# Latent attention with maxima computed one half-head ahead: values taken for four key tiles at a time

## The reference, cut to what matters

```python
q = rmsnorm(x @ q_a_w.T, q_a_ln) @ q_b_w.T            # 2048 tokens, 16 heads, 64 + 64 (rope)
ckv = x @ kv_a_w.T                                    # latent c (32) and one shared k_pe (64)
kv = rmsnorm(c, kv_a_ln) @ kv_b_w.T
query = concat([q_nope, rope(q_pe)]); key = concat([k_nope, rope(k_pe)])
scores = einsum('bhsd,bhtd->bhst', query, key) / sqrt(128)
attn = softmax(scores)                                # over all 2048 keys, no mask
out = einsum('bhst,bhtd->bhsd', attn, v)
return out.transpose(0, 2, 1, 3).reshape(B, S, H * VD) @ o_w.T
```

## Time and profile before

| | |
|---|---|
| median of three runs | 2275.55 us (2272.08 to 2276.42) |
| the profiled execution's own time | 2273.43 us |
| its span | 2271.2 us |
| TensorE busy | 2033.0 us, 90% of the span |
| VectorE, ScalarE, GpSimd busy | 1404.6, 1359.6 and 1356.0 us (60 to 62%) |
| mean granted TensorE clock | 0.938 of full |

### The profile page before, as it was taken

How to read it: one execution, slowest core, us unless ns; L and a number is a source line. 1 busy time by engine, 2 the same in 40 slices (tenths; PEclk the granted TensorE clock), 3 DMA queues, 4 the chain that set the end, 5 groups by cost and what they waited for, 6 DMA issues and landing times. The chain is left out here.

```text
span 2271.2 us, 44766 instructions
## 1 busy us (share of the span) xinstructions
PE 2033.0 (90%) x13754; PEld 1328.6 (58%) x13754; DVE 1404.6 (62%) x2973; ACT 1359.6 (60%) x1959; POOL 1356.0 (60%) x799
## 2 busy tenths in 40 slices
PE   5898999999999999999999999999764379999980
PEld 3653666666666666666666666666553257777760
DVE  4545777777776777777776777674242144555547
ACT  2421677777777777777777777778521025555540
POOL 1240678777777777777877778778443703333330
PEclk8886999999999999999999999999876689999995
DMA  4118993000000000000000000000011428999977
GB/s 166 43 44 315 403 400 118 0 0 0 0 0 0 0 0 0 0 0 0 0 0 0 0 0 0 0 0 2 27 59 52 144 78 278 347 337 336 334 265 259
DMA packets 90470, 227.44 MB, mean 100 GB/s; under 512 B 13198, under 2 KB 46904, under 8 KB 90296
## 3 DMA queue, kind: packets, MB, share of 16 engines
q1 hardware_dynamic: 77368, 195.03, 24.4%
q0 software_dynamic: 10752, 29.72, 3.4%
q10 hardware_dynamic: 2304, 2.10, 0.3%
HBM read 125.52 MB, written 101.28 MB: 100 GB/s over the span
## 5 line engine op out<-in xcount | busy, mean ns | idle before, releaser
L688 POOL TENSOR_TENSOR prob_lo<-prob,prob_hi 128x1024 f16<-128x1024 f32 x512 | 1092.5, 2156 | 336.3 <-ACT prob_hi L711 336.3
L760 DVE TENSOR_REDUCE maxes<-ring 128x1 f32<-128x512 f32 x1024 | 648.2, 685 | 245.5 <-PE ring L860 230.4
L709 ACT ACTIVATE prob<-p_s,prob_scale 128x1024 f32<-128x1024 f32 x512 | 571.1, 1115 | 361.9 <-PE p_s L894 361.6
L711 ACT ACTIVATE prob_hi<-p_s,prob_scale 128x1024 f16<-128x1024 f32 x512 | 569.7, 1113 | 0.0
L860 PE MATMUL ring<-kr_hi,qr_hi 64*128 64x512 f32 x1024 | 404.7, 417 | 9.9 <-DVE qc_hi L747 7.0
L860 PE MATMUL ring<-kc_pair,qc_hi 64*128 64x512 f32 x1024 | 387.6, 399 | 0.0
L894 PE MATMUL p_s<-qr_lo,kr_hi 64*128 64x512 f32 x1024 | 298.9, 391 | 0.0
L894 PE MATMUL p_s<-qr_hi,kr_lo 64*128 64x512 f32 x1024 | 297.2, 390 | 0.0
L1157 POOL DMA_INDIRECT ranked_out<-y,dest x128 | 122.6, 958 | 266.3 <-DVE y L1461 263.6
L894 PE MATMUL p_s<-qr_hi,kr_hi 64*128 64x512 f32 x1024 | 280.9, 435 | 0.3 <-ACT prob_hi L711 0.3
L894 PE MATMUL p_s<-qc_lo,kc_one 33*128 33x512 f32 x1024 | 252.9, 392 | 0.0
(11 more groups left out here) (240 smaller groups left out, 2805.6 us busy)
## 6 DMA issues: line engine op xcount, KB each, us to landing
w<-in_experts SPq DMA_DIRECT2D x128, 608.0 KB
expert_rows<-zeros SPq DMA_DIRECT2D x129, 526.0 KB, 9.1
rows<-expert_rows SPq DMA_DIRECT2D x128, 131.5 KB
got<-ranked_out SPq DMA_DIRECT2D x16, 768.0 KB, 11.1
wqb<-in_wqb SPq DMA_DIRECT2D x16, 341.0 KB, 3.0
x<-in_x SPq DMA_DIRECT2D x1, 2048.0 KB, 8.1
cbar<-in_woT SPq DMA_DIRECT2D x1, 2048.0 KB
ranked_out<-y,dest POOLq DMA_INDIRECT x128
```

What stands on the lines that cost most here:

```text
L688: gp.tensor_tensor(prob_lo[s % NB][:, :], prob[s % 2][:, :], prob_hi[s % NB][:, :], ALU.subtract).then_inc(lo_ready, 1)
L709: act.activation(prob[s % 2][:, :], p_s[s % 2][:, :], ACT.Exp, bias=prob_scale[:, :], scale=SCALE)
L711: act.activation(prob_hi[s % NB][:, :], p_s[s % 2][:, :], ACT.Exp, bias=prob_scale[:, :], scale=SCALE).then_inc(p_ready, 1)
L760: v.tensor_reduce(maxes[:, at:at + 1], bank[:, :], AX.X, ALU.max).then_inc(ring_used, 1)
```

## The change

The half-head becomes four groups in place of eight. Group g scores key tiles 4g + 2 to 4g + 5 and then weighs tiles 4g to 4g + 3. The maxima are laid out anew (8 in group 0, from round 8 on, 12 in group 1, 12 in group 2, none in group 3), the groups have 28, 32, 32 and 20 rounds. `turn` moves to round 8 of group 0, amid scores; `rows` to the head of group 3, right behind values; `rope` to round 6 of group 3, amid scores; `rest` stays right ahead of values, now those of tiles 12 to 15. The number of every kind of instruction stays the same, and so do the buffers: two score buffers, three ring banks, eight `prob_hi` and `prob_lo`. The bookkeeping of ring uses is written otherwise, to the same effect.

```diff
-        SLOTS = BATCH * len(PARTS)
-
-        MORE, LESS, NONE = ((0, 4, 7), (2, 5, 9)), ((1, 6), (3, 8)), ((), ())
-        MAX_AT = (MORE, LESS, MORE, MORE, LESS, MORE, NONE, NONE)
+        SLOTS = 4 * len(PARTS)
+
+        MAX_AT = (((8, 11, 14, 17), (10, 12, 15, 19)), ((0, 3, 7, 10, 13, 17), (2, 5, 8, 12, 15, 18)),
+                  ((0, 3, 6, 9, 12, 15), (1, 4, 7, 10, 13, 17)), ((), ()))
...
-                aside = {(1, 0): ("turn", not first), (6, 8): ("rows", more)}.get((g, len(rounds)))
+                aside = {(0, 8): ("turn", not first), (3, 0): ("rows", more), (3, 6): ("rope", after)}.get((g, len(rounds)))
...
-                        now.append(("score", c, BATCH * g + 2 + at[c] // len(PARTS), at[c] % len(PARTS)))
+                        now.append(("score", c, 4 * g + 2 + at[c] // len(PARTS), at[c] % len(PARTS)))
...
-            if after and g in (5, 6):
-                rounds.append([({5: "rope", 6: "rest"}[g], None, None, None)])
...
-                    for kt in range(BATCH * g, BATCH * g + BATCH):
+                    if g == 3 and after:
+                        project_rest(half, use_of(m, "rest"), ring[PLACE["rest"] % RING])
+                    for kt in range(4 * g, 4 * g + 4):
                         weigh(kt, m)
```

More of the change, by code:

```diff
@@ L54 @@
 RING = 3
-BATCH = 2
 class Chain:
@@ L612, in attention @@
                  (kc_one, qc_lo, KR))
-        SLOTS = BATCH * len(PARTS)
-        MORE, LESS, NONE = ((0, 4, 7), (2, 5, 9)), ((1, 6), (3, 8)), ((), ())
-        MAX_AT = (MORE, LESS, MORE, MORE, LESS, MORE, NONE, NONE)
-        BEGUN = [[sum(len(MAX_AT[i][c]) for i in range(g)) for c in range(2)] for g in range(len(MAX_AT))]
+        SLOTS = 4 * len(PARTS)
+        MAX_AT = (((8, 11, 14, 17), (10, 12, 15, 19)), ((0, 3, 7, 10, 13, 17), (2, 5, 8, 12, 15, 18)),
+                  ((0, 3, 6, 9, 12, 15), (1, 4, 7, 10, 13, 17)), ((), ()))
+        BEGUN = [[sum(len(MAX_AT[i][c]) for i in range(g)) for c in range(2)] for g in range(4)]
         def plan(g, first=False, more=True, after=True):
@@ L635, in plan, with use_of @@
                     elif at[c] < SLOTS:
-                        now.append(("score", c, BATCH * g + 2 + at[c] // len(PARTS), at[c] % len(PARTS)))
+                        now.append(("score", c, 4 * g + 2 + at[c] // len(PARTS), at[c] % len(PARTS)))
                         at[c] += 1
                 rounds.append(now)
-            if after and g in (5, 6):
-                rounds.append([({5: "rope", 6: "rest"}[g], None, None, None)])
-            return rounds
[L643 to L657, removed]
+            return rounds
+        MAXIMA = [(c, n) for g in range(4) for now in plan(g) for what, c, n, part in now if what == "max" and part == 1]
+        USES = 2 * MX + 4
+        PLACE = {"turn": 0, "rows": USES - 3, "rope": USES - 2, "rest": USES - 1}
+        PLACE.update({place: 1 + i for i, place in enumerate(MAXIMA)})
+        def use_of(m, what, gone=0):
+            return USES + USES * m + PLACE[what] - gone
         block = st.enter_context(nc.Block())
@@ L713, in head @@
                     if s == 3 and more:
-                        act.wait_ge(ring_mm, use_of(2 * h, "turn")[0] + 1)
+                        act.wait_ge(ring_mm, use_of(2 * h, "turn") + 1)
                         copy_wq(h + 1)
@@ L789, in half_head @@
                 m = 2 * h + half
-                state = (first, more, after)
+                gone = 0 if more else 2
                 if not first:
                     copy_out(m - 1)
-                for g in range(len(MAX_AT)):
+                for g in range(4):
                     for now in plan(g, first, more, after):
@@ L796, in half_head @@
                             if what == "max" and part == 1:
-                                maximum(c, n, m + 1, *use_of(m, (c, n), *state), (c, n) == MAXIMA[-1])
+                                maximum(c, n, m + 1, use_of(m, (c, n)), ring[PLACE[c, n] % RING], (c, n) == MAXIMA[-1])
                             elif what == "turn":
-                                turn(1 - half, h - (1 - half), *use_of(m, "turn", *state))
+                                turn(1 - half, h - (1 - half), use_of(m, "turn", gone), ring[-gone % RING])
                             elif what == "rows":
-                                rows(m + 1, 1 - half, *use_of(m, "rows", *state))
+                                rows(m + 1, 1 - half, use_of(m, "rows"), ring[PLACE["rows"] % RING])
                             elif what == "rope":
-                                project_rope(half, *use_of(m, "rope", *state))
-                            elif what == "rest":
-                                split(m + 2, half, *use_of(m, "rest", *state))
+                                project_rope(half, use_of(m, "rope"), ring[PLACE["rope"] % RING])
+                if after:
+                    split(m + 2, half, use_of(m, "rest"), ring[PLACE["rest"] % RING])
             step(v.tensor_copy(identr[:, :], ident[:, :]))
@@ L826, in _ @@
             copy_out(2 * H - 1)
-            turn(1, H - 1, use_of(2 * H - 1, "turn", more=False)[0] + 1, ring[-1 % RING])
+            turn(1, H - 1, use_of(2 * H - 1, "turn", 1), ring[-1 % RING])
         @block.tensor
@@ L920, in half_head @@
                             elif what == "score" and more:
-                                score(c, n - 16, part, m + 1, 1 - half, use_of(m, "rows", *state)[0])
+                                score(c, n - 16, part, m + 1, 1 - half, use_of(m, "rows"))
                             elif what == "max":
-                                maximum(c, n, part, m + 1, 1 - half, *use_of(m, (c, n), *state))
+                                maximum(c, n, part, m + 1, 1 - half, use_of(m, (c, n)), ring[PLACE[c, n] % RING])
                             elif what == "turn":
-                                turn(m - 1, *use_of(m, "turn", *state))
+                                turn(m - 1, use_of(m, "turn", gone), ring[-gone % RING])
                             elif what == "rows":
-                                rows(m + 1, *use_of(m, "rows", *state))
+                                rows(m + 1, use_of(m, "rows"), ring[PLACE["rows"] % RING])
                             elif what == "rope":
-                                project_rope(h + 1, half, *use_of(m, "rope", *state))
-                            elif what == "rest":
-                                project_rest(half, *use_of(m, "rest", *state))
-                    for kt in range(BATCH * g, BATCH * g + BATCH):
+                                project_rope(h + 1, half, use_of(m, "rope"), ring[PLACE["rope"] % RING])
+                    if g == 3 and after:
+                        project_rest(half, use_of(m, "rest"), ring[PLACE["rest"] % RING])
+                    for kt in range(4 * g, 4 * g + 4):
                         weigh(kt, m)
@@ L956, in _ @@
             half_head(H - 1, 1, more=False, after=False)
-            turn(2 * H - 1, use_of(2 * H - 1, "turn", more=False)[0] + 1, ring[-1 % RING])
+            turn(2 * H - 1, use_of(2 * H - 1, "turn", 1), ring[-1 % RING])
 def ffn(nc, a, x, ident, mod, wov, cbar, routing, slots_dram, ranked_dram, out):
```

## The result

The changed kernel takes 2411.03 us (median of four, 2408.69 to 2413.62), the one before 2273.82 beside it: a ratio of 1.0615, 95% interval 1.0596 to 1.0634, so 137 us slower. The forecast was 2365, slower by 90, and its range ended at 2385. The direction and most of the mechanism held, but the time lies outside the range.

A forecast was written before the change was run, and what follows sets the result against it. The prediction took TensorE, issuing without a pause, to bound the kernel until the last half-head. Its terms, -0.93 + 3.73 = +2.80 us a half-head, made +89.6 us over 32 half-heads: 2365 us, range 2325 to 2385.

The forecast's parts named there:

- TensorE paces the stage: In attention, until the last half-head, TensorE issues without a pause; one half-head lasts 43.44 us.
- The gain: TensorE's own work per half-head, from fewer crossings and moved single steps: -0.93 us (-1.25 to -0.61).
- a crossing: TensorE going from scores to values and back: idle gaps on both sides and a longer first round, 0.31 us.
- `turn` amid scores: Placing `turn` among score rounds in group 0 was to cost 0 to 0.31 us a half-head, taken as +0.16.
- The waits: TensorE's waits for exponentials 2.93, ring 0.25 and five restarts 0.55 in groups of four: +3.73 us a half-head.
- What stays hidden: GpSimd's remainders, `rows`, `split` and `copy_out` were to fit under other work, adding no wait.
- what would make me wrong: Signs: third and fourth tiles at TensorE's own pace, waits at `turn` (`copy_out` late), or L907 waiting for remainders.
- Crossings win: Rival: exponentials keep pace in attention, leaving only -0.93 x 32 = -30 us; faster, 2246 us; chance 0.06.
- VectorE's ring takes over: Rival: twelve reductions outlast 28 rounds in groups 1 and 2; 74 us more, about 2439 us; chance 0.05.
- The clock falls: Rival: group 3's 1.22 us wait lowers TensorE's clock each time; 178 us more, about 2540 us; chance 0.03.

## Why the prediction was right, and where it was wrong

- **TensorE paces the stage, 43.44 us a half-head**: right. Halving ScalarE's and GpSimd's work in the kernel before changed attention by 7 us of 1396, and the half-heads between the first and the last not at all (43.43 us).
- **The gain, -0.93 us**: right in size; a crossing measured 0.35 against 0.31, `rows` 0.16 against 0.16. `turn` amid scores was somewhat dearer (up to 0.18 with the ring's part).
- **The waits, +3.73 us**: right. Groups 0 to 3 without `turn`'s wait came to 46.04 us against 46.24, the fourth tile of group 3 to 1.23 against 1.22, and the waits go with the values in twos. Within group 2 (11.21 against 11.45 by the sum's terms) it fell out otherwise than computed: the third tile comes 0.23 us late (forecast 0.05), the fourth 0.31 at most (forecast 0.60).
- **What stays hidden**: this step failed, in its last sentence, that `split` and `copy_out` fit into the 2.7 us of values and the eight rounds ahead of `turn`. I summed only what follows `rest`, at the durations of before, and took VectorE to be free when `rest` lands. `rope` still lands as far ahead of `rest` (6.62 us, 6.23 before), but groups of four let the remainders of three tiles follow each other without a pause, and `rope`'s sum and the copy to qr_hi, which now run beside them, take 2.2 and 2.1 us in place of 0.7 and 1.2. So the copy ends at 1045.85, 1.70 us after `rest` has landed (1042.21 + 1.94 = 1044.15), and all behind it is late by as much. Without that, `copy_out` would have ended at about 1050.14 - 1.67 = 1048.47, and `turn` could have started 0.14 us later, just ahead of its own 1048.74: the cover that I had counted was real, but with 0.1 us to spare. It measured 1.54 and 1.95 us of wait, 51 us of the 137 over the 30 half-heads, of which I had none. I had named this wait as what would make me wrong, and left its price out of the range.
- **Crossings win**: out. With the exponentials halved the changed layout was slower than its base, with GpSimd's work halved too it was level but for 4.8 us. My threshold for it (the pair of passes done in 1.4 us) was wrong too: at 1.27 us VectorE and `rope`'s place in group 3 still held TensorE.
- **VectorE's ring takes over**: not as I put it. The waits of VectorE that cost came through `copy_out` and, once that was moved, through the first maxima's bank in group 0, not through the twelve reductions.
- **The clock falls**: out; 0.99 to 1.00 through the stage.

The waits for exponentials, `turn`'s wait and its cause were each removed by a run and are shown. That a step of VectorE stands until GpSimd's instruction is done is shown too, by the fixed 0.55 and 0.28 us behind it; that the two meet at a port is the explanation of the Trainium skill's page SBUF — State Buffer, Who interferes with whom, and no run here tests it.

## What to carry to other kernels

When work that separates two users of a buffer is put off, count the distance from the buffer's release to its next use again: here values behind every second tile had hidden 2.1 us of exponentials for 0.31 us of crossing. When a step moves, walk the whole queue of every engine that takes it up, from the moved step to the next one that somebody waits for, and ask what else then runs beside it: VectorE's durations were not constants but depended on GpSimd. And a saving on the bounding engine pays only as far as the next engine's chain has slack; half of the small gain of `rows` was lost until `copy_out` left VectorE.

## What was not expected of the hardware

The same VectorE instruction (128x512, two inputs in SBUF) took 0.69 us in one place and 2.27 in another, 3.3 times as long; with GpSimd's instructions half as long 1.28. A copy from SBUF to SBUF took 0.43, 1.18 and 2.15 us. Instructions that read PSUM kept their 0.68 to 0.69 us in all of these. The long durations are waits: a step that met a subtraction of GpSimd ended 0.55 us (two inputs) or 0.28 us (copy) after it, whenever in that subtraction it had begun, and the copy that came 0.03 us ahead of one took 0.43 us.
